# First attention: maxima units in other slots, parts reordered, last batch's scores on two bank pairs, other loads issued by SyncE behind its weights

## The reference, cut to what matters

```
q, k, v = heads(x @ Wq + bq), heads(x @ Wk + bk), heads(x @ Wv + bv)
y  = softmax(mask(q k^T * scale)) v          # causal, 256 x 256 per head
qc, kc, vc = heads(x @ Wcq + bcq), heads(ctx @ Wck + bck), heads(ctx @ Wcv + bcv)
y += softmax(qc kc^T * scale) vc             # 256 x 64 per head
x  = x + (y @ Wp + bp)
```

## Time and profile before

| | us |
|---|---|
| median of 3 runs | 1610.44 (1608.16 to 1612.09) |
| profiled execution | 1614.97 |
| its span in the profile | 1613.2 |
| TensorE (PE) busy | 1379.0 (85%) |
| VectorE (DVE) busy | 1014.7 (63%) |
| ScalarE (ACT) busy | 845.2 (52%) |
| GpSimd (POOL) busy | 602.3 (37%) |

### The profile page before, as it was taken

The page is one execution under the profiler, slowest core; times in us unless marked ns, Lnnn a source line. Parts: engine busy times, 40 slices in busy tenths (PEclk is TensorE's granted clock), DMA queues, the critical chain, the costliest instruction groups (busy, mean ns, idle before and its releaser), DMA issues. The chain is left out here.

```text
span 1613.2 us, 42818 instructions
## 1 busy us (share of the span) xinstructions
PE 1379.0 (85%) x17848; PEld 865.6 (54%) x17848; DVE 1014.7 (63%) x2314; ACT 845.2 (52%) x1295; POOL 602.3 (37%) x1042
## 2 busy tenths in 40 slices
PE   4788888888599999899999999886988888598595
PEld 2344445544244444455666665564766666477484
DVE  3577777775444454567777777635688887576132
ACT  1366666665355555547666666543455555242131
POOL 3245455442300002325555555332234443135244
PEclk9999999998799999999999999997999999799698
DMA  5000000000420000000000000001001111112351
GB/s 168 2 3 2 3 2 2 2 3 2 122 60 1 1 1 0 1 1 29 15 29 29 16 29 29 17 32 47 1 29 42 42 41 42 48 50 78 116 147 47
DMA packets 54513, 53.76 MB, mean 33 GB/s; under 512 B 9273, under 2 KB 48573, under 8 KB 54066
## 3 DMA queue, kind: packets, MB, share of 16 engines
q1 hardware_dynamic: 45170, 39.57, 8.2%
q10 hardware_dynamic: 6336, 5.35, 1.2%
q0 software_dynamic: 2816, 6.11, 1.1%
HBM read 20.34 MB, written 14.49 MB: 22 GB/s over the span
## 5 line engine op out<-in xcount | busy, mean ns | idle before, releaser
L1477 DVE TENSOR_REDUCE b_nm<-psum 128x4 f16<-128x1024 f32 x128 | 156.5, 1223 | 85.3 <-PE psum L1365 43.5
L654 ACT ACTIVATE a_prob<-psum 128x768 f32<-128x768 f32 (+1 forms) x160 | 136.5, 853 | 94.4 <-PE psum L420 91.2
L539 DVE TENSOR_REDUCE a_nm<-psum 128x4 f16<-128x1024 f32 (+1 forms) x96 | 117.6, 1225 | 49.4 <-PE psum L447 26.5
L707 POOL TENSOR_SCALAR_AFFINE_SELECT a_prob<-a_prob 128x512 f32<-128x512 f32 x128 | 81.8, 639 | 157.6 <-ACT a_prob L654 157.6
L1396 PE MATMUL psum<-b_QTh,b_KTh 32*128 32x256 f16 x512 | 71.6, 273 | 30.2 <-DVE b_nm L1477 28.3
L982 ACT ACTIVATE xo_sb<-psum,f_w_h_s 128x512 f32<-128x512 f32 x64 | 44.1, 688 | 82.4 <-PE psum L866 82.4
L1401 PE MATMUL psum<-b_KTh,b_QTh 32*128 32x256 f16 x512 | 71.0, 274 | 3.5 <-DVE b_nm L1477 3.5
L1396 PE MATMUL psum<-b_QTh,b_KTl 32*128 32x256 f16 x512 | 70.8, 269 | 0.0
L1396 PE MATMUL psum<-b_QTl,b_KTh 32*128 32x256 f16 x512 | 70.7, 269 | 0.0
L1401 PE MATMUL psum<-b_KTl,b_QTh 32*128 32x256 f16 x512 | 69.8, 269 | 0.0
L1401 PE MATMUL psum<-b_KTh,b_QTl 32*128 32x256 f16 x512 | 69.8, 269 | 0.0
(11 more groups left out here) (444 smaller groups left out, 4654.1 us busy)
## 6 DMA issues: line engine op xcount, KB each, us to landing
f_h_wh<-b_rden SPq DMA_DIRECT2D x64, 128.0 KB, 2.1
f_h_wh<-c_rden SPq DMA_DIRECT2D x64, 128.0 KB, 2.1
expert_in<-empty SPq DMA_DIRECT2D x8, 662.5 KB, 13.0
m_xt<-expert_in SPq DMA_DIRECT2D x8, 662.5 KB
m_w<-in_L_ffn_w_dram SPq DMA_DIRECT2D x16, 256.0 KB
out_dram<-m_send SPq DMA_DIRECT2D x8, 256.0 KB, 2.5
x_sb<-in_x_dram SPq DMA_DIRECT2D x4, 256.0 KB, 6.8
x_sb<-in_x_dram ACTq DMA_DIRECT2D x4, 256.0 KB, 8.7
```

The costliest lines, as they stand in the source:

```text
L539: nc.vector.tensor_reduce(out, psum[:, 2:4, :].rearrange("p i (a b) -> p i a b", a=groups), X, ALU.max, negate=True).then_inc(max_done, 1)
L654: nc.scalar.activation(prob[unit % 5][:, :, 0:width], psum[:, 0:2, 0:width], ACT.Exp, scale=SCALE).then_inc(exp_done, 1)
L707: nc.gpsimd.affine_select(out=diagonal, in_=diagonal, compare_op=ALU.is_ge, fill=0.0, base=0, pattern=[[0, 4], [1, P]], channel_multiplier ...
L1477: v.tensor_reduce(self.nm[:, :, :].rearrange("p t (j r) -> p j t r", r=32)[:, 2 * e:2 * e + 2, :, g], self.pr.psum[:, 2:4, :].rearrange("p ...
```

## The change

It does six things:
1. Two of the three clears of V move from GpSimd to VectorE.
2. SyncE waits for all 15 weight loads before it issues others; x pieces 1 to 7, the FFN weights and the context are all issued by SyncE, none by ScalarE.
3. The maxima m5, m6, m7 stand one slot later (slots -6, -5, -4; no maximum in slot -7), and the cross maxima m6 and m7 stand behind the projections of their unit, not in front.
4. Parts: "k" in slot -15 and "v" in -14 (they swap), e1 from 14 to 13, e2 from 16 to 13.
5. LayerNorm's statistics from slot -33 to -36, its rstd from -33 to -34, the second cast of q from -19 to -21.
6. Scores of the last batch alternate between the bank pairs (0, 1) and (2, 3), once all maxima are done, and wait for the exponential before last.

```diff
@@ -177,9 +177,12 @@
         m = self.tiles[name] = self.pr.sb(f"{self.tag}_w_{name}", shape, F32, self.mem)
         self.loads += [(m[...] if part is None else part(m), source) for part, source in pairs]
 
-    def start(self):
+    def start(self, engine=None):
         for to, source in self.loads:
-            self.pr.load(to, source, self.sem)
+            if engine:
+                engine.dma_start(to, source).then_inc(self.sem, 16)
+            else:
+                self.pr.load(to, source, self.sem)
 
     def arrived(self, engine):
         engine.wait_ge(self.sem, 16 * len(self.loads))
@@ -266,7 +269,7 @@
     s0 = pr.sem("a_init")
     cleared = [*(m[...] for m in V + Vc), tok[:, :, :, :, NM:], kctok[:, :, NM:]]
     for i, m in enumerate(cleared):
-        (nc.gpsimd if i < 3 else nc.vector).memset(m, 0.0).then_inc(s0, 1)
+        (nc.gpsimd if i < 1 else nc.vector).memset(m, 0.0).then_inc(s0, 1)
     nc.vector.wait_ge(s0, len(cleared))
     for i in range(3):
         nc.vector.memset(V[i][:, :, :, D:D + 1], 1.0)
@@ -276,6 +279,7 @@
     nc.vector.memset(kctok[:, :, NM:NM + 1], 1.0).then_inc(s0, 1)
     nc.vector.wait_ge(s0, len(cleared) + 1)
     pr.fence()
+    nc.sync.wait_ge(wload, 16 * 15)
     meanwhile()
 
     ln = LayerNorm(pr, "aln", 2, mem)
@@ -289,9 +293,9 @@
 
 
 
-    SLOT = {"z": -28, "q0": -20, "q1": -16, "v": -15, "k": -14, "qk0": -24, "kc": -13, "ck": -23, "cv": -13,
-            "qk1": -22, "nm": -3, "e0": 12, "e1": 14, "e2": 16, "e3": 18, "e4": 20}
-    MAXIMA = {m: m - 12 for m in range(M)}
+    SLOT = {"z": -28, "q0": -20, "q1": -16, "v": -14, "k": -15, "qk0": -24, "kc": -13, "ck": -23, "cv": -13,
+            "qk1": -22, "nm": -3, "e0": 12, "e1": 13, "e2": 13, "e3": 18, "e4": 20}
+    MAXIMA = {m: m - (12 if m < 5 else 11) for m in range(M)}
     FIRST, LAST = -4, B + 1
 
     def batches(n, u, slots):
@@ -316,6 +320,13 @@
               ("cross", 1, 0), ("cross", 0, 0)]
     quarters = lambda ap: ap.rearrange("p (h k d) -> p h k d", k=4, d=D)
     rows = lambda j: slice(W * j, W * j + W)
+
+    first_maxima = lambda n, u: [(m, batch) for m, batch in batches(n, u, MAXIMA) if maxima[m][0] != "cross"]
+    last_maxima = lambda n, u: [(m, batch) for m, batch in batches(n, u, MAXIMA) if maxima[m][0] == "cross"]
+
+    def score_bank(n, u):
+
+        return 2 * (u % 2) if n == B - 1 else 0
 
 
     def tensor_drained(use):
@@ -407,23 +418,27 @@
         q, k, kc = QT[n % 3], KT[n % 3], KcT[n % 3]
         if u == 0:
             nc.tensor.wait_ge(nm_placed, 64 * (n + 1))
-        if n or u:
+        first = score_bank(n, u)
+        if n == B - 1 and u:
+            nc.tensor.wait_ge(max_done, M * B)
+            nc.tensor.wait_ge(exp_done, U * n + u - 1)
+        elif n or u:
             nc.tensor.wait_ge(exp_done, U * n + u)
         if u < 8:
             g, e = divmod(u, 2)
             for i in range(2):
                 r = rows(2 * e + i)
-                nc.tensor.matmul(psum[:, i, 0:T], k[r, g, 0:P], q[r, 0, g, :], start=True, stop=True,
+                nc.tensor.matmul(psum[:, first + i, 0:T], k[r, g, 0:P], q[r, 0, g, :], start=True, stop=True,
                                  skip_group_check=True)
             for i in range(2):
                 r = rows(2 * e + i)
-                inst = nc.tensor.matmul(psum[:, i, T:T + P], k[r, g, P:T], q[r, 0, g, P:T], start=False, stop=True,
+                inst = nc.tensor.matmul(psum[:, first + i, T:T + P], k[r, g, P:T], q[r, 0, g, P:T], start=False, stop=True,
                                         skip_group_check=True)
         else:
             for g in range(G):
                 for i in range(2):
                     r, half = rows(2 * (u - 8) + i), slice(TC * (g % 2), TC * (g % 2) + TC)
-                    inst = nc.tensor.matmul(psum[half, i, (g // 2) * T:(g // 2) * T + T], kc[r, g, :], q[r, 1, g, :],
+                    inst = nc.tensor.matmul(psum[half, first + i, (g // 2) * T:(g // 2) * T + T], kc[r, g, :], q[r, 1, g, :],
                                             start=(g < 2), stop=True, skip_group_check=True)
         inst.then_inc(st_full, 1)
 
@@ -499,7 +514,7 @@
             for u in range(U):
                 if 0 <= n < B:
                     tensor_scores(n, u)
-                for m, batch in batches(n, u, MAXIMA):
+                for m, batch in first_maxima(n, u):
                     tensor_max(batch, m)
                 if u in (3, 5, 7, 9) and 0 <= n < B:
                     tensor_values(n, u // 2 - 1)
@@ -507,6 +522,8 @@
                     tensor_values(n - 1, G)
                 for use in projections(n, u):
                     tensor_projection(use)
+                for m, batch in last_maxima(n, u):
+                    tensor_max(batch, m)
 
 
     def vector_normed(n, k):
@@ -596,12 +613,14 @@
     def vector_program():
         for n in range(FIRST, LAST + 1):
             for u in range(U):
-                for m, batch in batches(n, u, MAXIMA):
+                for m, batch in first_maxima(n, u):
                     vector_max(batch, m)
                 for use in projections(n, u):
                     if DRAIN[use[0]] == "v":
                         vector_projection(use)
-                for k, batch in batches(n, u, {0: -33, 1: -29}):
+                for m, batch in last_maxima(n, u):
+                    vector_max(batch, m)
+                for k, batch in batches(n, u, {0: -36, 1: -29}):
                     vector_normed(batch, k)
                 if n == B - 1 and u in (2, 5):
                     ffn.vector_normed(0, u // 5)
@@ -651,7 +670,8 @@
         if unit >= 5:
             nc.scalar.wait_ge(av_done, freed(unit))
         width = T + P if u < 8 else 2 * T
-        nc.scalar.activation(prob[unit % 5][:, :, 0:width], psum[:, 0:2, 0:width], ACT.Exp,
+        first = score_bank(n, u)
+        nc.scalar.activation(prob[unit % 5][:, :, 0:width], psum[:, first:first + 2, 0:width], ACT.Exp,
                              scale=SCALE).then_inc(exp_done, 1)
 
     def scalar_values(n, use):
@@ -667,7 +687,7 @@
                     scalar_scores(n, u)
                 for use, batch in batches(n, u, {0: 9, 1: 11, 2: 12}):
                     scalar_values(batch, use)
-                for t, batch in batches(n, u, {0: -22, 1: -19}):
+                for t, batch in batches(n, u, {0: -22, 1: -21}):
                     scalar_high(batch, t)
                 for use in projections(n, u):
                     if DRAIN[use[0]] == "a":
@@ -712,7 +732,7 @@
             for u in range(U):
                 if u < 8 and 0 <= n < B:
                     gpsimd_select(n, u)
-                for _, batch in batches(n, u, {0: -33}):
+                for _, batch in batches(n, u, {0: -34}):
                     ln.gpsimd_rstd(batch)
                 for _, batch in batches(n, u, {0: -24}):
                     gpsimd_context(batch)
@@ -2498,10 +2518,10 @@
 
         def others(f):
             for i in range(1, 8):
-                x_piece((nc.sync, nc.scalar)[i % 2], i)
-            f.start()
+                x_piece(nc.sync, i)
+            f.start(nc.sync)
             for a in range(2):
-                nc.scalar.dma_start(pr.ctx2[TC * a:TC * a + TC, :, :], io["ctx"]).then_inc(pr.ctx2_in, 16)
+                nc.sync.dma_start(pr.ctx2[TC * a:TC * a + TC, :, :], io["ctx"]).then_inc(pr.ctx2_in, 16)
 
         x_piece(nc.sync, 0)
         nc.scalar.dma_start(pr.ctxT[:, :, :], io["ctxT"]).then_inc(pr.ctxT_in, 16)
```

## The result

The changed kernel takes 1569.04 us (median of 4 runs, 1566.71 to 1576.64) against 1609.34 for the kernel before (4 runs, 1608.16 to 1612.09): ratio 0.9755, 95% interval 0.9729 to 0.9782. The prediction was 1574.0, range 1564 to 1594.

A forecast was written before the change was run, and what follows sets the result against it. TensorE's queue bounds the steady periods, ScalarE's load issues the start. Start 11.3, batch 0 1.2, twelve periods 19.2, batches 13 and 14 2.2, last batch 1.0, tail 1.5: 36.4 us off 1610.44 gives 1574.0, range 1564 to 1594.

The forecast's parts named there:

- Memsets, barrier, ScalarE's copy: Kernel start: barrier 1.48 us earlier, statistics near 6.45, first z copied at 9.67, first qk at 10.7; 6.2 us won.
- rival B: Start: loads hold it, with a late x piece delaying V's drain and late weights; total 1578.6 us; chance 0.08.
- Up to the first maximum and to nm: Batch 0's start: first maximum 13.05 us after first qk, 3.05 won; from there to nm 2.4 won.
- P: The prediction's own theory: separate gains from the start, TensorE's five waits per period (limited by transfers) and the ends.
- The steady period: Twelve periods, batches 1 to 13: each 20.7 instead of 22.35 us, limited by nm's transfers; 19.2 us won.
- the four waits: TensorE's waits in units 3 to 6 of a period, 0.40, 0.35, 0.21 and 0.57: all go, 1.53 us.
- The m1 wait's removal buys nothing: Steady period: a 0.54 us wait before a maximum falls to about 0.15, without gain, since scores wait for nm's transfers.
- Last batch: Last batch's scores: second bank pair removes exponential waits, 1.0 us, but gives nothing at half clock, where TensorE is full.
- Tail: End of the first attention: third epilogue part's reciprocal goes before the FFN's normalisation on VectorE; stage ends 1.5 us earlier.
- A: Steady period: VectorE becomes the bound and each period slips by 0.8 us; total 1583.6 us; chance 0.20.
- C: Steady period: it doesn't move, as transfer latency takes back every gain; 17.2 us left, 1593.2 us; chance 0.05.
- D: Steady period: the new wait before scores costs TensorE's clock, 59 us over twelve periods; total 1632.8 us; chance 0.05.

The follow-up runs named there:

- loads_mixed: Changed kernel with x pieces, FFN weights and context issued in turn by SyncE and ScalarE, without SyncE's wait for the weights; 1580.37 us, ratio 0.9804.
- start_only: Kernel before with only the new start (two V clears on VectorE, loads on SyncE behind the weights), old order, one bank pair; 1602.61 us, ratio 0.9947.
- one_move: Changed kernel with nm's four row transfers of a batch made as one transfer; 1569.68 us, ratio 0.9750.
- ctx_one: Changed kernel with GpSimd's context copy three units earlier and nm's four rows in one transfer; 1559.52 us, ratio 0.9688.
- banks_only: Kernel before with only the second pair of score banks in the last batch added; 1607.27 us, ratio 0.9974.
- ctx_early: Changed kernel with GpSimd's copy of the context three units earlier, slot -27 instead of -24; 1561.64 us, ratio 0.9688.
- stats_back: Changed kernel with LayerNorm's statistics and rstd back in slot -33; 1569.05 us, ratio 0.9755.
- no_banks: Changed kernel with one bank pair for the last batch's scores, as before; 1576.17 us, ratio 0.9793.
- e_back: Changed kernel with the two epilogue parts that had moved to slot 13 back in slots 14 and 16; 1570.78 us, ratio 0.9764.
- after_again: Changed kernel run once more without any edit; 1568.27 us, ratio 0.9745 to the kernel before.
- clears_back: Changed kernel with two clears of V back on GpSimd; 1570.14 us, ratio 0.9745.

## Why the prediction was right, step by step

**The time came out (1569.0 for 1574.0), the sum of its terms less so.** Six terms gave 36.4, the profiles 44.5. Nearly all the missing 8 us lie in terms that contain stretches at half clock, and the range held it.

*Memsets, barrier, ScalarE's copy.* Right to 0.03 us (6.48 for 6.45, 9.68 for 9.67). The first qk at 11.34 is the latest of the nine profiles with this start and these clears; they run from 10.29 to 11.34, and their median is 10.70, the value taken. Free for SyncE: right, it was through at 22.4, and pieces landed in 2.9 to 5.2 us; rival B is out. What was mis-sized was the value for the kernel before: its 16.89 was the low end of 16.9 to 20.1 (loads_mixed). The Trainium skill ("DMA: Bandwidth & Descriptors", section "Issuing engines are not separate DMA queues") says that more issuing engines save only issue time. The runs agree: the pieces from one queue landed in 2.9 to 5.2 us, not later than the 3.4 to 13.6 from two. It also calls the issue time usually small relative to the DMA itself. That helps little here: ScalarE's eleven issues together took 8.5 us before and up to 13.2 (loads_mixed), all in front of its first work, and moving them was worth 7 us (start_only, with the clears) to 12 (loads_mixed).

*Up to the first maximum and to nm.* 4.27 and, to the scores, 5.41, where I had 3.05 and 2.4. What the order does was right; I had used the durations of before, and they didn't stay. The first maximum was to stand 13.05 us behind the first qk, and in the three profiles with the whole new order in which its group of four still takes 0.61 us, as before, it stands at 12.95 to 12.98 (loads_mixed, one_move, ctx_one). In the other seven, the changed kernel's among them, the group takes 0.39 us and the maximum stands at 11.3 to 12.5. So of the 4.27 us some 3.1 are the order and 1.2 the clock. When the clock rises here isn't a matter of the order: banks_only, in the old order, has 0.39 too.

From there to nm all eleven profiles of the new order take 18.9 to 21.0 us, the three of the old one 23.9 to 24.2. Here the rise does go with the order. m7 of batch 0, first in the kernel before, then in the changed kernel:

```profile
51.36 0.61 PE L464 MATMUL psum<-a_KcT,a_QT 32*128 32x64 f16 x16 [0.51 <-DVE a_nm L534]
```

```profile
39.94 0.40 PE L479 MATMUL psum<-a_KcT,a_QT 32*128 32x64 f16 x16
```

That group takes 0.61 us in all three profiles of the old order and 0.40 or 0.41 in all eleven of the new one. The waits that P named are gone with it, 1.41 us before m6 and 0.51 before m7. TensorE is busy 13.40 us for 119 matmuls over the whole way, before 17.36 for 120, but this difference isn't a gain of its own size: banks_only is busy 15.50 us and still takes 23.88. So P's 2.4 were the waits, and by these durations the rest of the 5.3 is the clock. The same holds for batch 0's period (3.14 for 1.2): the kernel before had half-clock durations in it until about 74, and among the kernels with the new maxima it varies from 20.4 to 23.8. The granted clock column reads 1.00 in these first stretches of the kernel before, so durations had to be read, and I had not asked what the clock would do with fewer waits in front of it.

*The steady period.* 20.57 for 20.7, nm at offset 15.99 for 15.98, nm to scores 4.59 for 4.72, the wait for the transfers 0.49 for 0.65. The term is right, but one step failed: "nothing of note, so nm stands at 15.98". In the kernel before kc stood at 16.29:

```profile
213.95 0.29 PE L368 MATMUL psum<-ident,a_kctok 64*128 64x64 f16 x4
```

Less the 1.53 us of the four waits that is 14.76. TensorE was at kc at 14.03, and then waited 0.84 for the context's copy. The first error: I took out the four waits by their listed lengths, 1.53 us. The work of a period shrank too, from 19.71 to 19.00 for the same matmuls; a group that starts without a wait runs into its neighbours (m7 at 121.26, the scores at 121.40, m7's last six at 121.42), and a wait costs TensorE its length and the overlap behind it. The second: of GpSimd I had said only that statistics "come earlier"; I never laid its queue out for units 5 and 6, where split, select and rstd fill it (ctx_early, stats_back). The two errors are equal by accident. Without the second the change would have given 7 us more (ctx_early).

"The m1 wait's removal buys nothing" was right in its result, but not for the reason given alone: with the transfers' limit away (one_move), m1's reduction is at the same place. Moving the statistics cost 0.35 us a period and won 3.7 at the start (stats_back).

*Batches 13 and 14*: 2.66 for 2.2, no error that a run can tell. *Last batch*: 1.0 was too low; the runs give 4.2 (banks_only) and 7 (no_banks). "The second pair gives nothing there" was argued from TensorE being full at the half clock until 405, but the half clock ends after 5 us in start_only, with the same order and banks, so the argument leaned on the clock of one profile. With the clock back as early the pair is worth 1.55 us in the old order; in the new order it removes 1.9 us of waits, and the half clock 12.5 to 15 us behind the scores, which both kernels with one pair have, doesn't come. *Tail*: 1.5 for 2.1 by e_back, 1.76 of it the shorter wait for y. (2.1 and 5.7 are more than the 4.67 of the table, since the last batch without the pair takes longer in the new order than in the old.)

*Rivals.* A is out as it was put: no reduction releases TensorE at m5 to m7. But VectorE is level with the transfers (one_move), and would take over from them. C is out. D, the slower case, didn't come at its size. But the prediction named as a sign of being wrong that the granted clock leaves 1.00 between batch 1 and 13, and it did, once in the twelve periods (0.99 over the whole stretch):

```profile
189.54 0.64 PE L441 MATMUL psum<-a_QT,a_KcT 32*64 32x256 f16 x8
...
195.41 0.28 PE L431 MATMUL psum<-a_QT,a_KT 32*128 32x256 f16 x2
```

From about 188.5 to 195 durations are those of the 1.2 GHz level, with TensorE busy throughout; the periods there are 21.64 and 21.43, 1.9 us more than two of 20.57. It was batch 7 again in after_again, but batch 9 in no_banks, the same program there. In these stretches the three profiles of the old order have no fall; of the eleven of the new order six have one or more (clears_back between 149 and 173 us and again between 277 and 301) and five none. one_move has one (batch 6) though no transfer holds its scores, so that the new wait before the scores costs the clock, as D has it, isn't shown. What the falls cost is: about 2 us in 249 instead of the 59 of D.

## What to carry to other kernels

When a wait is removed, lay out the queue of every engine that works for the next instruction, not only the one that was named: here GpSimd, idle for 47% of the twelve periods, hid a copy that came 0.8 us late eleven times. A removed wait gave its length here and, where matmuls overlap or TensorE stood at half clock, more. Read durations, since they tell the clock's level where the granted clock column doesn't. And loads issued by a computing engine at the start cost it all the time until its queue takes them: 8.5 to 13.2 us for the same eleven in four profiles. Last, before a term is argued from the clock of one stretch of one profile, look whether another profile of the same part has that clock: the half clock from the last batch's first scores ended after 5 us in some kernels and after 10 in others, with one bank pair and with two.

## What the runs showed of the hardware that I had not expected

- Two DMA issues at the end of ScalarE's queue of 11 took 1.23, 3.46, 4.01 and 4.54 us in four profiles, and ScalarE computed nothing meanwhile.
- Packets of a queue of the kind "instruction" (q14) beside small transfers: in batches 3 to 14 of the changed kernel nm's four rows took 4.8 to 5.2 us where one or two such packets fell between them, 4.58 to 4.59 elsewhere at full clock. One transfer of the same four rows took 4.02 to 4.03 with or without such a packet, but for one batch of one_move (5.54), where the clock had fallen.
- The granted clock column reads 1.00 in the first 70 us of the kernel before, while its matmuls have the durations of the half clock (0.61 for the group that takes 0.39 later).
- VectorE's clear of 1024 f32 columns took 0.91 us; four times its clear of 256 is 1.09.
- With a second bank pair in the kernel before, TensorE was back at full speed 4.5 us after the last batch's first scores, without it after 10; in the changed order one pair brought a second fall that two did not.
